# Moving the row maxima and half of the f32 probabilities of an attention stage into PSUM, and two weight operations from GpSimd to ScalarE

## The reference, cut to what matters

```python
x = x + _L0_xattn_ref(_layernorm(x), ctx_1024, ...)        # first attention, one head
x = x + _L0_ffn_ref(_layernorm(x), L0_ffn_rhs)             # int8-like product
# second attention, 16 heads of 32: the stage that is changed
q, k, v = heads(_layernorm(x) @ w_q.T), heads(ctx @ w_k.T), heads(ctx @ w_v.T)
attn = softmax(einsum("bqhd,bkhd->bhqk", q, k) * 32 ** -0.5)
x = x + einsum("bhqk,bkhd->bqhd", attn, v).reshape(B, T_q, 512) @ w_o.T
x = x + _L1_ffn_ref(_layernorm(x), ...)                    # shared expert and 8 routed experts
```

## Time and profile before

| What | us |
|---|---|
| median of 3 runs | 1278.62 (1277.63 to 1279.98) |
| the profiled execution | 1274.63 |
| its span, first to last instruction | 1272.9 |
| TensorE busy | 1181.6 (93%) |
| VectorE busy | 962.6 (76%) |
| ScalarE busy | 651.4 (51%) |
| GpSimd busy | 579.1 (45%) |

### The profile page before, as it was taken

How to read it: one execution, slowest core, us unless ns; L and a number is a source line. 1 busy time by engine, 2 the same in 40 slices (tenths; PEclk the granted TensorE clock), 3 DMA queues, 4 the chain that set the end, 5 groups by cost and what they waited for, 6 DMA issues and landing times.

```text
span 1272.9 us, 28618 instructions
## 1 busy us (share of the span) xinstructions
PE 1181.6 (93%) x10708; PEld 801.4 (63%) x10724; DVE 962.6 (76%) x2080; ACT 651.4 (51%) x1183; POOL 579.1 (45%) x698
## 2 busy tenths in 40 slices
PE   6888997679999999988899999999999999999997
PEld 3555654567777777776444444677777777666663
DVE  5889898879999999986486867777776776645451
ACT  4377787657767777765445232122222222465653
POOL 0047677646556666643110000354644355377744
PEclk9999999999999999999899999999999999999999
DMA  9521023123444544453494041214031502699987
GB/s 344 205 67 68 1 32 45 43 84 107 165 140 153 170 142 168 160 152 106 166 183 92 1 111 55 68 34 100 1 100 35 166 2 69 195 254 249 251 145 99
DMA packets 159608, 150.49 MB, mean 118 GB/s; under 512 B 80592, under 2 KB 113520, under 8 KB 159472
## 3 DMA queue, kind: packets, MB, share of 16 engines
q1 hardware_dynamic: 138432, 121.75, 33.4%
q0 software_dynamic: 14400, 25.35, 9.9%
q10 hardware_dynamic: 6640, 1.58, 0.7%
HBM read 84.93 MB, written 57.19 MB: 112 GB/s over the span
## 4 chain that ended last, share of the span: by engine, by line
PE 77%; DVE 13%; issue 3%; ACT 2%; DMA 2%; POOL 1%; ACTq 1%; SPq 0%; DVEq 0%; POOLq 0%
PE bank L124 25%; PE bank L2234 14%; PE bank L2227 13%; PE bank L1599 6%; PE bank L980 3%; DVE att_land L1276 3%; PE bank L1553 3%; PE bank L1530 2%; PE bank L1506 2%; DVE att_land L1269 2%; PE bank L1049 1%; PE bank L897 1%; DMA att_land<-att_land 1%; PE bank L1546 1%; PE bank L916 1%
## 5 line engine op out<-in xcount | busy, mean ns | idle before, releaser
L1732 POOL DMA_INDIRECT lists<-att_land x128 | 134.1, 1047 | 294.9 <-DVE att_land L1873 168.8
L2227 PE MATMUL bank<-att_land 128*128 128x512 f16 x768 | 176.2, 379 | 0.0
L124 PE MATMUL bank<-program_xs,program_wgu 128*128 128x512 f16 x576 | 128.9, 379 | 0.6 <-DVE att_land L1832 0.6
L2227 PEld LDWEIGHTS bank<-att_land 128*128 128x128 f16 x768 | 75.1, 98 | 81.7
L2055 ACT ACTIVATE att_land<-program_x 128x512 f32<-128x512 f32 x40 | 25.2, 631 | 195.1 <-DVE program_x L2197 195.1
L124 PE MATMUL bank<-att_land 128*128 128x128 f16 (+1 forms) x1560 | 106.0, 221 | 3.0 <-DVE att_land L1333 3.0
L1599 PE MATMUL bank<-att_land 128*128 128x512 f16 x384 | 106.2, 389 | 1.7 <-DVE att_land L1354 1.7
L1217 POOL TENSOR_TENSOR att_land<-att_land 120x512 f16<-120x512 f32 x64 | 74.3, 1161 | 68.9 <-ACT att_land L1409 68.9
L124 PEld LDWEIGHTS bank<-program_xs,program_wgu 128*128 128x128 f16 x576 | 56.0, 98 | 67.3 <-DVE att_land L1832 1.1
L1269 DVE TENSOR_REDUCE att_land<-bank 128x4 f32<-128x480 f32 x128 | 83.6, 653 | 17.4 <-PE bank L1506 14.2
L124 PEld LDWEIGHTS bank<-att_land 128*128 128x128 f16 x1560 | 89.3, 98 | 5.8 <-DVE att_land L1333 3.4
(11 more groups left out here) (321 smaller groups left out, 3010.8 us busy)
## 6 DMA issues: line engine op xcount, KB each, us to landing
xn_rows<-att_land SPq DMA_DIRECT2D x37, 256.0 KB, 2.8
out_rows<-att_land SPq DMA_DIRECT2D x37, 256.0 KB, 6.2
att_land<-q_rows SPq DMA_DIRECT2D x66, 128.0 KB, 2.7
q_rows<-att_land SPq DMA_DIRECT2D x32, 256.0 KB, 2.3
xt_tiles<-att_land SPq DMA_DIRECT2D x32, 256.0 KB, 2.1
x_rows<-program_x SPq DMA_DIRECT2D x8, 1024.0 KB, 4.9
att_land<-x_rows SPq DMA_DIRECT2D x8, 1024.0 KB, 6.0
program_xs<-xt_tiles SPq DMA_DIRECT2D x28, 256.0 KB, 5.5
```

The source lines that it names most:

```text
L124: last = pe.matmul(out, lhs(a, k), rhs(b, k), start=n == 0, stop=n == len(terms) - 1)
L1732: pool.indirect_dma_start(out=io["lists"], out_offset=bass.IndirectOffsetOnAxis(ap=index[:, t, k:k + 1], axis=0), in_=load[:, t, k, :], in ...
L2227: last = pe.matmul(ps_y[i][:, :], hid[:, c % 2, a, i * P:(i + 1) * P], wd[:, q, c, :], start=c == 0 and n == 0, stop=c == NC - 1 and n == 2)
```

## The change

- `nmax` moves from SBUF to the last 16 columns of bank 1 in PSUM. The high part of the maxima is made with `tensor_scalar` in place of `scalar_tensor_tensor` with a broadcast constant.
- For chunks 2 and 3 the f32 exponential is no longer written to SBUF: ScalarE first writes the f16 high half and then the f32 exponential in place over the bank, and VectorE subtracts from the bank. For chunks 0 and 1 nothing changes. So ScalarE's order for chunk 3 becomes high half, f32 exponential, `shift_rows`, where it was f32 exponential, `shift_rows`, high half.
- TensorE waits for the low halves of chunks 2 and 3 of the tile before (`p_last`) ahead of writing banks 2 and 3 anew.
- Parts 0 and 1 of the weights go to ScalarE (`weights_high`, at the end of its step, behind `gate_high`); part 2 stays on GpSimd.
- Some places in `JOIN` move; the only one that puts work of `attention1` behind other live work is ScalarE's (1, 1), the exponentials of tile 0, chunk 1, from 70 to 73.

```diff
-    prob = g.early(7 * D, [P, KC, HC * P])
+    prob = g.early(7 * D, [P, LOWS, HC * P])
-    nmax = small("nmax", [P, KC, HC])
+    nmax = banks[1][:, HC * J:HC * J + HEADS].rearrange("p (c h) -> p c h", c=KC)
 # GpSimd, weights(t): parts 0 and 1 removed
-            if part == 0:
-                pool.wait_ge(w_in, 16 * (b + 1))
...
-                pool.tensor_tensor(raw[:, :], raw[:, :], g.ws[:, :].to_broadcast([P, IS]), ALU.mult)...
-            elif part == 1:
-                need(pool, w_part, 3 * b + 1)
-                pool.tensor_tensor(g.wgu[:, b, 0, :], raw[:, :], g.one[:, :].to_broadcast([P, IS]), ALU.mult)...
-            else:
+            if part == 2:
 # VectorE
-                dve.scalar_tensor_tensor(high, nmax[:, :], 1 / NS, g.one[:, 0:1].rearrange("p (o n) -> p o n", o=1)
-                                         .to_broadcast([P, KC, HC]), ALU.mult, ALU.mult).then_inc(s["shift"], 1)
+                dve.tensor_scalar(high, nmax[:, :], 1 / NS, None, ALU.mult).then_inc(s["shift"], 1)
-                dve.wait_ge(c4["p_hi"], KC * u + c + 1)
-                dve.tensor_tensor(pT[0:J, c, 1], prob[0:J, c], pT[0:J, c, 0], ALU.subtract).then_inc(c4["p_last"], 1)
+                dve.wait_ge(c4["exp"], KC * u + c + 1)
+                dve.tensor_tensor(pT[0:J, c, 1], ps_t[c % 2][0:J, :], pT[0:J, c, 0], ALU.subtract).then_inc(c4["p_last"], 1)
 # ScalarE, exps(u, c)
-            if u > 0:
-                lows_done(act, u - 1, c)
-            act.activation(prob[0:J, c], ps_t[c % 2][0:J, :], ACT.Exp).then_inc(c4["exp"], 1)
+            if c < LOWS:
+                if u > 0:
+                    lows_done(act, u - 1, c)
+                act.activation(prob[0:J, c], ps_t[c % 2][0:J, :], ACT.Exp).then_inc(c4["exp"], 1)
+                prob_high(u, c)
+            else:
+                prob_high(u, c)
+                act.activation(ps_t[c % 2][0:J, :], ps_t[c % 2][0:J, :], ACT.Exp).then_inc(c4["exp"], 1)
+        def weights_high(t):
+            b, part = divmod(t - 4, 3)
+            if not 0 <= b < B or part == 2:
+                return
+            if part == 0:
+                act.wait_ge(w_in, 16 * (b + 1))
...
+                act.activation(raw[:, :], raw[:, :], ACT.Copy, scale=WS).then_inc(w_part.handle, 1)
+            else:
+                need(act, w_part, 3 * b + 1)
+                act.activation(g.wgu[:, b, 0, :], raw[:, :], ACT.Copy).then_inc(w_part.handle, 1)
             exps(t - 1, 3)
             shift_rows(t)
-            prob_high(t - 1, 3)
             gate_high(t - 4)
+            weights_high(t)
 # TensorE, scores_transposed(u, c)
-            need(pe, c4["p_hi"], KC * u + c - 1)
+            if c >= 2:
+                need(pe, c4["p_hi"], KC * u + c - 1)
+            else:
+                need(pe, c4["p_last"], 2 * (u - 1) + c + 1)
 # JOIN["scalar"], the one place with live work on both sides
-(1, 1): 70
+(1, 1): 73
```

More of the change, by code:

```diff
@@ L1228, in weights @@
                 return
-            if part == 0:
-                pool.wait_ge(w_in, 16 * (b + 1))
[L1231 to L1234, removed]
-            elif part == 1:
-                need(pool, w_part, 3 * b + 1)
-                pool.tensor_tensor(g.wgu[:, b, 0, :], raw[:, :], g.one[:, :].to_broadcast([P, IS]), ALU.mult).then_inc(w_part.handle, 1)
-            else:
+            if part == 2:
                 need(pool, w_part, 3 * b + 2)
@@ L1397, in exps @@
             act.wait_ge(c4["t_mm"], KC * u + c + 1)
-            if u > 0:
-                lows_done(act, u - 1, c)
-            act.activation(prob[0:J, c], ps_t[c % 2][0:J, :], ACT.Exp).then_inc(c4["exp"], 1)
+            if c < LOWS:
[6 more added lines that the diff above has]
+                act.activation(ps_t[c % 2][0:J, :], ps_t[c % 2][0:J, :], ACT.Exp).then_inc(c4["exp"], 1)
         def prob_high(u, c):
-            if not live(u):
-                return
             need(act, c4["o_mm"], KC * (u - 1) + c + 1)
@@ L1409, in prob_high @@
             act.activation(pT[0:J, c, 0], ps_t[c % 2][0:J, :], ACT.Exp).then_inc(c4["p_hi"], 1)
+        def weights_high(t):
[4 more added lines that the diff above has]
+                act.wait_ge(w_in, 16 * (b + 1))
+                if b == 0:
+                    act.wait_ge(f.a["s_mm"], NT)
+                    act.wait_ge(f.a["y_mm"], NT)
+                act.activation(raw[:, :], raw[:, :], ACT.Copy, scale=WS).then_inc(w_part.handle, 1)
+            else:
+                need(act, w_part, 3 * b + 1)
+                act.activation(g.wgu[:, b, 0, :], raw[:, :], ACT.Copy).then_inc(w_part.handle, 1)
         def shift_copied(u):
@@ L1660, in attention1 @@
         s[n] for n in ("q_mm", "q_lo", "xt_mm", "y_mm", "of", "g_tr", "g_lo", "l_mm", "l_ok", "n_ok"))
-    done.t_mm, done.p_hi, done.o_mm = (c4[n] for n in ("t_mm", "p_hi", "o_mm"))
+    done.t_mm, done.p_last, done.o_mm = (c4[n] for n in ("t_mm", "p_last", "o_mm"))
     return done
@@ L2249, in tensor @@
             if v == 1:
-                need(pe, t.p_hi, KC * NT)
+                need(pe, t.p_last, 2 * NT)
             matmuls(pe, ps_g[c % 2][:, :], lambda a, k: g.wgu[:, k, a, c * P:(c + 1) * P],
@@ L2592, in experts @@
     return sync, gpsimd, scalar, vector, tensor
[L2595 to L2597 removed]
+JOIN = {"sync": {(-6, 0): 60, (-6, 1): 67},
+    "gpsimd": {(-6, 0): 45, (-6, 1): 45, (-6, 2): 47, (-6, 3): 47, (-5, 0): 49, (-5, 1): 49, (-5, 2): 49, (-5, 3): 49, (-4, 0): 50, (-4, 1): 50, (-4, 2): 53, (-4, 3): 53, (-3, 0): 53, (-3, 1): 53, (-3, 2): 53, (-3, 3): 53, (-2, 0): 54, (-2, 1): 54, (-2, 2): 57, (-2, 3): 57, (-1, 0): 61, (-1, 1): 61, (-1, 2): 61, (-1, 3): 61, (0, 0): 65, (0, 1): 65, (0, 2): 66, (0, 3): 66, (1, 0): 70, (1, 1): 72, (1, 2): 73, (1, 3): 73, (2, 0): 73, (2, 1): 73, (2, 2): 73, (2, 3): 73, (3, 0): 78, (3, 1): 78, (3, 2): 80, (3, 3): 80, (4, 0): 80, (4, 1): 83},
+    "scalar": {(-6, 0): 49, (-6, 1): 49, (-6, 2): 49, (-6, 3): 52, (-5, 0): 52, (-5, 1): 54, (-5, 2): 54, (-5, 3): 54, (-4, 0): 54, (-4, 1): 54, (-4, 2): 54, (-4, 3): 54, (-3, 0): 54, (-3, 1): 54, (-3, 2): 54, (-3, 3): 54, (-2, 0): 59, (-2, 1): 59, (-2, 2): 61, (-2, 3): 61, (-1, 0): 61, (-1, 1): 61, (-1, 2): 63, (-1, 3): 63, (0, 0): 65, (0, 1): 65, (0, 2): 69, (0, 3): 69, (1, 0): 70, (1, 1): 73, (1, 2): 79, (1, 3): 79, (2, 0): 79, (2, 1): 79, (2, 2): 79, (2, 3): 79, (3, 0): 80, (3, 1): 81},
```

3 lines of the change are left out of this document (removed).

## The result

The changed kernel takes 1258.66 us (median of 4 runs, 1257.06 to 1265.29) where the kernel before, run beside it, takes 1278.12 (4 runs, 1275.85 to 1279.98). The ratio is 0.986, with a 95% interval of 0.9834 to 0.9885: 17.9 us less, between 14.7 and 21.2. Predicted were 1259.9 and 18.7 less. The profiled execution took 1257.52 us with a span of 1255.7, 17.2 less than before; predicted were 1255.9 and 1254.2.

The account below looks back on a forecast made before the run. TensorE was taken as the bound, with VectorE's stall added; 17.9 + 0.5 + 5.9 + 0.9 - 5 - 0.5 - 1 = 18.7 us less, median 1278.6 to 1259.9, own range 1254 to 1265.

Parts of the forecast that it names:

- The hold: VectorE's high part of the shifts, held by GpSimd's weight operation, drops to 0.2 us; TensorE's transpose wait goes, 17.9 us gained.
- Rival B: VectorE stays held in the 8 tiles with GpSimd's remaining subtraction; only 11.5 us less, 1267.1; chance 0.08.
- Order of chunk 3: ScalarE's earlier high half lets VectorE's subtraction and TensorE's `outputs` start sooner: 2.4 us mid-stage, 3.5 at the ends, 5.9 gained.
- tile 1: High part of the shifts in this early tile was held as well; freeing it gives 0.46 us.
- JOIN: At the stage's start ScalarE does `front`'s last rounding before two exponentials, 0.96 us sooner; TensorE's wait shrinks, 0.9 us gained.
- The price of the order: Shift-row transfers issued one ScalarE slot later, 0.48 us; paid mainly in 8 weight tiles, 5 us lost; bounds 0 and 15.
- Rival A: Shift-row transfers become the wait of every tile, 0.4 us in 24 tiles; only 9.1 us less, 1269.5; chance 0.16.
- Weights on ScalarE: 16 weight operations of 1.1 us on ScalarE, nearly swallowed by the waits of `query_high` and `rows_high`; 0.5 us lost.
- rival C: No change: ScalarE takes VectorE's place, its weight copies cost full price, 17.6 us; 1.1 us less, 1277.5; chance 0.08.
- Subtraction from PSUM, exponential in place: VectorE's 64 subtractions reading PSUM: from -30 to 0 ns each, on an engine with slack; counted as nothing.
- rival D: Slower: chunk 3's in-place exponential delays the shift rows' issue; at 2.5 us each, 16 us slower, 1295; chance 0.03.
- Query loads: Shorter pitch leaves query loads less time; one more wait likely in batches with the big x_rows store; 1 us lost.

Follow-up runs that it names:

- e11: Kernel before with tensor_scalar for the high part of the maxima, its one input left in SBUF; 1281.06 us, ratio 1.0009.
- e3: Kernel before with only the chunk 2 and 3 probabilities in PSUM and the new exponential order; maxima and weights as before; 1273.86 us, ratio 0.9968.
- e4: Changed kernel with GpSimd's 512 KB weight block fetch moved into its next step; 1264.15 us, ratio 0.9892 to the kernel before.
- e5: Changed kernel with GpSimd's weight block fetch held until the f32 exponential of chunk 3 is made; 1255.59 us, ratio 0.9814 to the kernel before.
- e6: Changed kernel with both shift rows sent in one 8 KB transfer instead of two of 4 KB; 1249.36 us, ratio 0.9756 to the kernel before.
- e1: Kernel before with only the maxima in PSUM and tensor_scalar for the high part; weights stay on GpSimd; 1263.68 us, ratio 0.9896.
- e8: Changed kernel with parts 0 and 1 of the weights back on GpSimd; 1258.52 us, ratio 0.9843 to the kernel before.

## Why the prediction was right

- **The hold.** Right in place and cause: high part at 0.19 us everywhere, L1513's wait gone. Its size was short. I took the waits that the view shows, 17.9 us in 24 tiles (16.7 in the 23 of the account); the tiles lost 21.3 over their undisturbed pitch. A wait of 0.5 to 1.0 us cost its tile 0.8 to 1.1. The reason was too narrow: one input in SBUF is enough to hold a tensor_scalar, as e11 shows. Rival B falls: L1269 has at most 198 ns beside L1231.
- **Order of chunk 3.** I put 0.1 of the 0.2 us a tile into TensorE's pitch. It is all of it: 10.26 to 10.06, 4.6 us in 23 tiles instead of 2.3 (e3 alone: 3.7). At the ends I had 3.5, plus 0.5 for tile 1 and 0.9 for JOIN. The L1041 wait is gone, and tiles 0 to 3 are 2.9 shorter, but the first transpose isn't earlier. In the profiles of the variants it lies between 246.8 and 250.8, so 0.9 can't be read there. Of the 5.2 us of waits for the subtraction at the ends 1.7 are left, the 3.5 less that I had, but tiles 26 to 31 gave 0.3 only: two waits of 4.0 us together for query rows stand there.
- **The price of the order: the step that failed.** "The two shift transfers are issued one ScalarE slot later" is false: T + 0.64 both times. The loss I drew from it was real and mis-sized, 9.5 us of waits from 290 to 545 against 5 (12.2 in what tiles 3 to 25 lost by them), and its cause is another: the moment T moved against GpSimd's subtraction, so that the block fetch behind it falls on the second transfer (e4, e5), and the pair has no slack (e6). e1 shows it without any new order. That GpSimd's fetch "moves the same way" I had as a reason for a loss of nothing; it doesn't move with T, since GpSimd no longer holds VectorE back. Rival A was half right: the waits stand in 12 tiles of 23, not in all. That the quiet tiles keep 0.8 us of slack was wrong for those in which an instruction packet meets the second transfer.
- **Weights on ScalarE.** 1.05 us for 1.1, swallowed by L1435's and L1441's waits; rival C falls: from 290 to 545 us TensorE has no wait for ScalarE. I gave the move no gain and 0.5 us of loss. e8, without it, has the change's time, so neither shows.
- **Subtraction from PSUM, exponential in place.** 593 ns in place, and rival D falls. The subtraction takes 672 ns from PSUM against 688 from SBUF: beside TensorE either way. The Trainium skill has the opposite sign (VectorE: DVE Perf Modes, the table of errata-adjusted costs, where PSUM is the dearer source); the measurement decides, and here PSUM is not dearer.
- **Query loads.** 1 us expected; 1.5 in the middle and 4.0 from 545 to 610, against 1.7 before, so 3.8 more.
- **Behind the stage** I had nothing, and 2.8 us went there. The 41 us behind the transpose of tile 31 had a granted clock of 0.92 before and have 1.00 now; the other kernels' times from there to the end lie between 669.8 and 674.1. So this can be chance as well as the change.

Put together: the stall gave 4.6 more than its term and the order 2.3 more; the new waits of the middle cost 13.9 where I had about 6. Two errors of 7 and 8 us met with opposite signs. The ends gave 2.6 us (2.9 + 0.3 - 0.65) where I had 4.9, and the 2.8 behind the stage made up for them. That the medians fell within 1 us of the forecast is luck; that the hold went, and why, is not.

## What to carry to other kernels

A short VectorE instruction on the path that ends 0.05 us behind a GpSimd instruction every time is held by it; here an operand in PSUM freed it, and then moving GpSimd's work away bought nothing. When a stall goes that tied two engines together, list what was issued behind it and where that traffic falls now. A transfer that the path waits for every tile should be one transfer: here that was worth 9 us more after the change and 11 on the kernel before, by the medians, for a few lines.

## What the runs showed of the hardware

ScalarE's queue issues a DMA while an ACTIVATE ahead of it in the program still waits or runs: L1428 starts at 401.69, L1395, ahead of it in the program, at 402.17.

4 KB transfers land after 1.7 us in tiles where no other packet meets theirs. The second of the pair lands after 3.3 to 3.8 us behind one 16 KB instruction packet (tiles 7, 10, 13, 16, 23) and after 3.5 to 4.3 in the tiles with the 512 KB fetch, and its last packet ends within 0.06 us of theirs each time. What counts is not its size but what its packets stand behind.

A tensor_scalar of 128x16 with a single input in SBUF was held beside GpSimd (1214 ns in the median of e11, 1766 at most); with that input in PSUM none was (e1, 197 at most).

A wait of 2.5 us costs TensorE more than itself. In e6 the wait for query rows at 389.43 (2.48 us) makes a tile of 14.12 us, 4.05 over the undisturbed 10.07. The stretches around it (columns as in the earlier trace rows, the granted clock third from the end):

```profile
384.00:388.00 4.00, 2.94 (x74) 2.83 (x70) 2.94 (x8) 3.12 (x5) 1.96 (x6) 1.00 0.40 112
388.00:392.00 4.00, 2.58 (x15) 2.03 (x16) 1.72 (x3) 1.10 (x3) 0.00 (x0) 0.62 0.17 60
```

TensorE stands from 386.95 to 389.43. The clock is still granted almost in full from 388 to 389 (0.98) and is 0.50, the lower of its two levels (1.2 GHz), from 389 to 392, while TensorE resumes; from 392 to 393 it is 0.82. In tile 15 of the change a wait of 1.32 costs 1.53 (411.15 to 422.75). From 355 to 405 us the granted clock was 0.93 in e4, where such long waits stand, and 1.00 in the change. So e4's long waits weigh more than their sum: its waits from 290 to 545 us are 14.8, and its tiles 3 to 26 take 26 us more than undisturbed ones (257.66 against 231.5).
